# Folded wide cross attention in a two-layer decoder: scores issued three half tiles ahead in place of two

## The chip, the core and the metric

The kernel runs on one core of a Trainium2 chip. The metric is the device time of one execution, in microseconds. The engines are TensorE (PE, with PEld its weight loads), VectorE (DVE), ScalarE (ACT), GpSimd (POOL) and SyncE (SP, which issues the transfers). Each has its own instruction stream; they wait for one another by semaphores.

## What is computed

A decoder of two layers on x (4 batches of 512 tokens, 128 wide) with a context of 77 tokens per batch. Each layer is self attention, cross attention and a mixture of eight experts, and behind each an addition and a layer norm. The change lies in the cross attention of the second layer: 16 heads of 64 over the 77 context tokens.

```python
def _L1_xattn_ref(inputs_q, inputs_kv, Wq, bq, Wk, bk, Wv, bv, Wo, bo):
    q = jnp.einsum('bqm,mhd->bqhd', inputs_q, Wq) + bq
    k = jnp.einsum('bkm,mhd->bkhd', inputs_kv, Wk) + bk
    v = jnp.einsum('bkm,mhd->bkhd', inputs_kv, Wv) + bv
    q = q / jnp.sqrt(jnp.asarray(HD, q.dtype))
    attn = jax.nn.softmax(jnp.einsum('bqhd,bkhd->bhqk', q, k), axis=-1)
    out = jnp.einsum('bhqk,bkhd->bqhd', attn, v)
    return jnp.einsum('bqhd,hdm->bqm', out, Wo) + bo
...
x = _layernorm(x + _L1_xattn_ref(x, ctx_1024, ctx_1024, ...), axis=-1)
```

## The kernel before

`decoder` runs the stages one after another. Ahead of `flat_cross`, `wide_operands` has folded the projections: A holds for each batch and head Wq times the keys, CP the part that comes from the query bias (three bf16 parts), U the values times Wo. So scores are XT times A, and the output is the weights times U, with no projection of x in between.

`flat_cross` handles 16 tiles of 128 tokens (NT), each in two halves of eight heads (HH): 32 half tiles h, with tile t = h // 2 and batch t // 4. The program of each engine is written out without a loop on the chip, and its order is the order of the Python calls. For one half tile:

- PE `score(h)`: two groups of four heads, each a matmul of XT with A (L1876, f32, 308 columns) and one that adds CP (L1878), into the two banks of ps_s chosen by h % 2. Ahead of them it waits for `lessened` of h - 2, which read those banks.
- DVE `lessen(h)`: maximum of each head (L1961), then the subtraction from PSUM into PR[h % RING] (L1965). RING is 3, so it waits until PE has turned h - 3.
- ACT `exp(h)` (L1926), in place in PR.
- DVE `total(h)`: sum (L1972) and reciprocal (L1976).
- POOL `normalise(h)` (L1853): PR times the reciprocal, in place.
- PE `turn(h)`: five transposes of PR into the two banks of ps_t (L1886), after `normed` of h and `taken` of h - 1.
- ACT `take(h)` (L1932): ps_t into PT[h % 2].
- PE `weigh(h)`: PT times U into ps_v or ps_f by tile (L1896; the profile shows ten instructions for five matmuls).
- DVE `add(t)` (L1982): the output added to X, once per tile.

Once per batch the layer norm follows in the midst of the next batch: DVE `statistics` (L1986, L1989) in its iteration with h % 8 == 2, POOL `rstd` (L1847, L1849), DVE `apply` (L1995) in the iteration with h % 8 == 3, then PE `back` (L1904, four transposes of X into the first bank of ps_t, behind `s_n`) and ACT `columns` (L1939, from there to XT). Since `back` uses a bank of ps_t, the next turn waits for `s_xt`. The last batch's runs behind the loop.

What sets the order around the change is the order within each program: DVE's iteration h is lessen(h + 2), total(h + 1), the addition and the step of the layer norm; ACT's is take(h), exp(h + 2); POOL's is normalise(h), with rstd behind that of h % 8 == 3; PE's is in the lines below. SP issues one small load for this stage (L1830).

Of the kernel before, what the change touches and what calls it, by code (L numbers as in the profile page):

```python
# [14 lines left out]
QT = S // P  # L15
# [1767 lines left out]
def flat_cross(c, tag, A, CP, U, bo, pre=None):  # L1783
# [6 lines left out]
    HALVES = 2 * NT  # L1790
    HH = H // 2
    W = CHUNKS * P
    RING = 3
    norms = 1 if pre is None else 2
    with ExitStack() as own:
        ONES = c.sb(f"{tag}_ONES", [NPART, P], BF16, own)
        BO = c.sb(f"{tag}_BO", [P, P], F32, own)
        WB = c.sb(f"{tag}_WB", [P, 2], F32, own)
        PR = c.sb(f"{tag}_PR", [P, RING, W], F32, own)
        PT = c.sb(f"{tag}_PT", [P, 2, W], F32, own)  # L1800
# [14 lines left out]
        def heads(ap):  # L1815
            return ap.rearrange("p (h k) -> p h k", k=KC)
# [4 lines left out]
        def output(t):  # L1821
            return (c.ps_v, c.ps_f)[t % 2][:, (t // 2 % 4) * P:(t // 2 % 4 + 1) * P]
# [4 lines left out]
        with nc.Block() as block:  # L1827
            @block.sync
            def _(sp):
                sp.dma_start(BO[:, :], row(bo)).then_inc(s_w, 16)  # L1830
                if pre is not None:
                    sp.dma_start(WB[:, 0:1], col(pre[0])).then_inc(s_w, 16)
                    sp.dma_start(WB[:, 1:2], col(pre[1])).then_inc(s_w, 16)

            @block.gpsimd
            def _(pool):
# [14 lines left out]
                def normalise(h):  # L1851
                    pool.wait_ge(inverted, h + 1)
                    nc.gpsimd.tensor_tensor(  # L1853
                        heads(PR[:, h % RING, 0:HH * KC]), heads(PR[:, h % RING, 0:HH * KC]),
                        RDEN[:, h % 2, :].rearrange("p (h a) -> p h a", a=1).broadcast_to([P, HH, KC]),
# [10 lines left out]
            @block.tensor  # L1866
            def _(pe):
                def score(h):
                    t, half = h // 2, h % 2
                    b = t // QT  # L1870
                    if h >= 2:
                        pe.wait_ge(lessened, h - 1)
                    for q in range(2):
                        g = slice(half * HH + 4 * q, half * HH + 4 * q + 4)
                        dst = c.ps_s[:, 2 * (h % 2) + q, 0:4 * KC]
                        nc.tensor.matmul(dst, c.XT[:, t * P:(t + 1) * P], A[:, b, g, :].rearrange("p h k -> p (h k)"),  # L1876
                                         start=True, stop=False)
                        mm = nc.tensor.matmul(dst, ONES[:, :], CP[:, g, b, :], start=False, stop=True)  # L1878
                    mm.then_inc(scores, 1)

                def turn(h):
                    pe.wait_ge(normed, h + 1)
                    if h >= 1:
                        pe.wait_ge(taken, h)
                    for i in range(CHUNKS):
                        mm = nc.tensor.transpose(c.ps_t[:, i // 4, (i % 4) * P:(i % 4 + 1) * P],  # L1886
                                                 PR[:, h % RING, i * P:(i + 1) * P], c.ident[:, :])
                    mm.then_inc(turned, 1)

                def weigh(h):  # L1890
                    t, half = h // 2, h % 2
                    pe.wait_ge(taken, h + 1)
                    if half == 0 and t >= 2:
                        pe.wait_ge(summed_x, t - 1)
                    for i in range(CHUNKS):
                        mm = nc.tensor.matmul(output(t), PT[:, h % 2, i * P:(i + 1) * P], U[:, t // QT, half * CHUNKS + i, :],  # L1896
                                              start=(half == 0 and i == 0), stop=(half == 1 and i == CHUNKS - 1))
                    mm.then_inc(weighed, 1)

                def back(b):  # L1900
                    pe.wait_ge(s_n, QT * (b + 1))
                    for i in range(QT):
                        src = c.X[:, b * QT + i, :] if pre is None else R2[:, i, :]
                        mm = nc.tensor.transpose(c.ps_t[:, 0, i * P:(i + 1) * P], src, c.ident[:, :])  # L1904
                    mm.then_inc(s_back, 1)

                pe.wait_ge(s_ones, 1)
                pe.wait_ge(s_pad, 1)
                score(0)
                score(1)  # L1910
                for h in range(HALVES):
                    if h % (2 * QT) == 6 and h > 6:
                        pe.wait_ge(taken, h)
                        back(h // (2 * QT) - 1)
                        pe.wait_ge(s_xt, h // (2 * QT))
                    turn(h)
                    if h + 2 < HALVES:
                        score(h + 2)
                    weigh(h)
                back(B - 1)  # L1920

            @block.scalar
            def _(act):
                def exp(h):
                    act.wait_ge(lessened, h + 1)
                    nc.scalar.activation(PR[:, h % RING, 0:HH * KC], PR[:, h % RING, 0:HH * KC], ACT.Exp).then_inc(exped, 1)  # L1926

                def take(h):
                    act.wait_ge(turned, h + 1)
                    if h >= 2:  # L1930
                        act.wait_ge(weighed, h - 1)
                    nc.scalar.activation(PT[:, h % 2, :], c.ps_t[:, :, :].rearrange("p a n -> p (a n)")[:, 0:W],  # L1932
                                         ACT.Copy).then_inc(taken, 1)

                def columns(b):
                    act.wait_ge(s_back, b + 1)
                    dst, src = c.XT[:, b * S:(b + 1) * S], c.ps_t[:, 0, :]
                    if pre is None:
                        nc.scalar.activation(dst, src, ACT.Copy).then_inc(s_xt, 1)  # L1939
                    else:  # L1940
                        nc.scalar.activation(dst, src, ACT.Identity, bias=WB[:, 1:2], scale=WB[:, 0:1]).then_inc(s_xt, 1)

                act.wait_ge(s_w, n_w)
                exp(0)
                exp(1)
                for h in range(HALVES):
                    if h % (2 * QT) == 6 and h > 6:
                        columns(h // (2 * QT) - 1)
                    take(h)
                    if h + 2 < HALVES:  # L1950
                        exp(h + 2)
                columns(B - 1)

            @block.vector
            def _(dve):
                stat, done = Chain(s_stat), Chain(s_n)

                def lessen(h):
# [3 lines left out]
                    dve.wait_ge(maxed, h + 1)  # L1962
                    if h >= RING:
                        dve.wait_ge(turned, h - RING + 1)
                    nc.vector.tensor_tensor(  # L1965
# [332 lines left out]
def decoder(nc, a, out):  # L2298

    scratch = nc.dram_tensor("split_parts", (B, 2, P, NPART, S), BF16, kind="Internal").ap()  # L2300
    with ExitStack() as ctx:
# [29 lines left out]
        with ExitStack() as own:  # L2331
            A, CP, U = flat_operand_tiles(c, "e", own)
            wide_operands(c, "e", *(a[f"L1_xattn_{n}"] for n in ("Wq", "bq", "Wk", "bk", "Wv", "bv", "Wo")), A, CP, U)
            flat_cross(c, "e", A, CP, U, a["L1_xattn_bo"])
# [33 lines left out]
```

## Time and profile before

| | us |
|---|---|
| median of 3 runs | 2390.18 |
| lowest, highest | 2387.64, 2396.96 |
| the profiled execution: time | 2394.99 |
| its span | 2393.2 |
| busy in the span: PE, PEld | 1842.1, 1041.4 |
| DVE, ACT, POOL | 1385.4, 1035.7, 155.9 |

The mean granted clock of TensorE over the span is 0.866 of full. The folded cross attention runs from 1920 us (its first scores) to 2175 us in this span. Matmuls are pipelined and their ends are modelled: a busy PE isn't PE at its peak, and neighbouring groups can overlap by a little.

### The profile page before, as it was taken

How to read it: one execution, taken by the hardware profiler on the slowest of the kernel's cores; microseconds unless marked ns; L12 is line 12 of the kernel's file. 1: busy time of each engine (PE TensorE's matmuls, PEld its weight loads, DVE VectorE, ACT ScalarE, POOL GpSimd, SP SyncE). 2: the span in 40 equal slices, each digit the busy share in tenths (PEclk: the TensorE clock that was granted, in tenths of full speed). 3: DMA queues.
4: the chain of work that ended last, by engine and by line, in shares of the span. 5: the costliest groups of instructions: out<-in, count | busy, mean ns of one | idle time of the engine just before them, and what ended most of it. 6: DMA issues, size and time to landing. Idle time of an engine off the chain costs nothing. (4 is left out here: it accounts for less than half of the span.)

```text
span 2393.2 us, 33578 instructions
## 1 busy us (share of the span) xinstructions
PE 1842.1 (77%) x9665; PEld 1041.4 (44%) x9718; DVE 1385.4 (58%) x4754; ACT 1035.7 (43%) x1970; POOL 155.9 (7%) x281
## 2 busy tenths in 40 slices
PE   3277773873365867799949999999999677777997
PEld 2144442541022323577724444544444345455665
DVE  7398866656365754433358777777677433333445
ACT  3288861651054645334316556566556221111221
POOL 2000003001000000000020000000000021110000
PEclk7699995896588989899969999999999865766999
DMA  2543102402513110100010000000000100000000
GB/s 56 79 46 36 18 3 42 58 11 47 78 13 39 21 21 3 36 19 18 10 36 1 1 1 1 1 1 0 1 1 1 36 2 1 1 0 14 21 20 24
DMA packets 57636, 48.74 MB, mean 20 GB/s; under 512 B 12691, under 2 KB 53047, under 8 KB 57527
## 3 DMA queue, kind: packets, MB, share of 16 engines
q1 hardware_dynamic: 57527, 47.45, 12.5%
q8 instruction: 49, 0.80, 0.1%
q14 instruction: 60, 0.49, 0.1%
HBM read 38.30 MB, written 8.91 MB: 20 GB/s over the span
## 5 line engine op out<-in xcount | busy, mean ns | idle before, releaser
L1432 PE MATMUL ps_s<-d_KZ,d_Q 128*128 128x512 f32 x512 | 265.4, 601 | 16.1 <-issue 6.8
L1580 ACT ACTIVATE d_PR<-d_PR,d_NM 128x512 f32<-128x512 f32 x256 | 184.6, 721 | 189.8 <-DVE d_NM L1511 189.3
L557 DVE TENSOR_REDUCE c_NM<-ps_t 128x1 f32<-128x512 f32 x256 | 169.9, 688 | 99.2 <-PE ps_t L437 97.5
L1507 DVE CUSTOM_DVE_ANT_0 d_PR<-ps_s,d_BH 128x512 f32<-128x512 f32 x256 | 176.2, 688 | 61.6 <-PE ps_t L1440 44.7
L437 PE MATMUL ps_t<-KX,QX 96*128 (+1 forms) x256 | 107.6, 425 | 108.7 <-DVE c_IB L575 47.9
L1440 PEld LDWEIGHTS ps_t<-ident,d_PR 128*128 128x128 f32 x1024 | 121.4, 141 | 150.7 <-issue 132.5
L619 ACT ACTIVATE c_PT<-ps_s 128x1024 f32<-128x1024 f32 x128 | 130.4, 1024 | 128.6 <-PE ps_s L460 126.7
L2282 DVE SCALAR_TENSOR_TENSOR X<-ps_t,GATE,X 128x128 f32<-128x128 f32 x272 | 76.7, 344 | 184.2 <-PE ps_t L2207 184.2
L1587 ACT ACTIVATE d_PT<-ps_t 128x512 f32<-128x512 f32 x256 | 149.9, 586 | 50.7 <-PE ps_t L1440 49.0
L1440 PE MATMUL ps_t<-ident,d_PR 128*128 128x128 f32 x1024 | 156.4, 275 | 10.1 <-ACT d_PT L1587 8.1
L762 ACT ACTIVATE a_PR<-a_PR,a_NM 128x128 f32<-128x128 f32 (+3 forms) x256 | 129.8, 555 | 77.9 <-DVE a_NM L743 77.9
L672 PE MATMUL ps_t<-ident,a_PR 128*128 128x128 f32 x640 | 115.5, 290 | 50.4 <-ACT a_PT L686 38.0
L2244 ACT ACTIVATE f_HT<-ps_s,f_BE 128x512 f32<-128x512 f32 x128 | 87.8, 687 | 128.0 <-PE ps_s L2197 127.2
L2197 PE MATMUL ps_s<-XT,g_W 128*128 128x512 f32 x288 | 132.5, 603 | 2.4 <-DVE g_HT L2261 2.4
L1519 DVE TENSOR_SCALAR d_PR<-d_PR,d_RDEN 128x512 f32<-128x512 f32 x256 | 124.7, 487 | 9.0
L2207 PEld LDWEIGHTS ps_t<-f_W,f_HT 128*128 128x128 f32 x1024 | 119.2, 192 | 14.8 <-issue 14.6
L1452 PE MATMUL ps_v<-d_PT,d_VB 128*64 128x512 f32 x512 | 116.9, 598 | 5.6 <-ACT d_PT L1587 5.0
L2207 PE MATMUL ps_t<-f_W,f_HT 128*128 128x128 f32 x1024 | 119.3, 275 | 0.0
L2197 PE MATMUL ps_s<-XT,f_W 128*128 128x512 f32 x256 | 117.0, 601 | 0.0
L1961 DVE TENSOR_REDUCE e_M<-ps_s 128x8 f32<-128x616 f32 x32 | 25.6, 800 | 153.0 <-PE ps_s L1878 153.0
L672 PEld LDWEIGHTS ps_t<-ident,a_PR 128*128 128x128 f32 x640 | 70.3, 142 | 96.2 <-ACT a_PT L686 48.1
L437 PEld LDWEIGHTS ps_t<-KX,QX 96*128 (+1 forms) x256 | 25.0, 98 | 187.3 <-issue 105.9
(330 smaller groups left out, 3237.6 us busy)
## 6 DMA issues: line engine op xcount, KB each, us to landing
QX<-split_parts SPq DMA_DIRECT2D x108, 128.0 KB
KX<-split_parts SPq DMA_DIRECT2D x72, 128.0 KB
f_W<-in_L_ffn_w SPq DMA_DIRECT2D x16, 256.0 KB, 3.1
split_parts<-a_PARTS SPq DMA_DIRECT2D x8, 384.0 KB, 10.0
split_parts<-c_PARTS SPq DMA_DIRECT2D x8, 384.0 KB, 11.2
g_W<-in_L_ffn_w SPq DMA_DIRECT2D x24, 128.0 KB, 2.2
split_parts<-b_PARTS SPq DMA_DIRECT2D x4, 384.0 KB, 10.7
X<-in_x SPq DMA_DIRECT2D x4, 256.0 KB
```

The source lines that it names most:

```text
L437: nc.tensor.matmul(c.ps_t[:, i % 2, :], QX[0:SROWS, bass.ds(head, 1), qt * P:(qt + 1) * P], KX[0:SROWS, bass.ds(head, 1), :], start=True, ...
L557: nc.vector.tensor_reduce(NM[:, qt, j:j + 1], c.ps_t[:, i % 2, :], AX.X, ALU.max, negate=True).then_inc(maxed, 1)
L619: nc.scalar.activation(PT[:, half, j, :, :], c.ps_s[:, 2 * (j % 2):2 * (j % 2) + 2, :], ACT.Exp).then_inc(exped, 1)
L672: last = nc.tensor.transpose(c.ps_t[:, qt % 2, kt * P:(kt + 1) * P], PR[:, j % 2, qt, kt * P:(kt + 1) * P], c.ident[:, :])
L762: nc.scalar.activation(PR[:, j % 2, qt, 0:k], PR[:, j % 2, qt, 0:k], ACT.Exp, bias=NM[:, j % 2, qt:qt + 1]).then_inc(exped, 1)
L1432: nc.tensor.matmul(c.ps_s[:, qt % 2, :], Q[:, p % 2, qt * P:(qt + 1) * P], KZ[:, p % 2, i % 2, :], start=True, stop=True).then_inc(scores, 1)
L1440: mm = nc.tensor.transpose(c.ps_t[:, qt % 2, kt * P:(kt + 1) * P], PR[:, i % 2, qt, kt * P:(kt + 1) * P], c.ident[:, :])
L1507: nc.vector.tensor_tensor_reduce(out=PR[:, h % 2, qt, :], in0=c.ps_s[:, qt % 2, :], in1=BH[:, h, S - P - qt * P:2 * S - P - qt * P], scale ...
L1580: nc.scalar.activation(PR[:, h % 2, qt, :], PR[:, h % 2, qt, :], ACT.Exp, bias=NM[:, h % 2, qt:qt + 1], accum_out=DEN[:, h % 2, qt:qt + 1] ...
L1587: nc.scalar.activation(PT[:, i // 2 % 2, i % 2, :, qt * P:(qt + 1) * P], c.ps_t[:, qt % 2, :].rearrange("p (k q) -> p k q", q=P), ACT.Copy ...
L2197: nc.tensor.matmul(c.ps_s[:, ch, :], W[:, (ch % CH) * P:(ch % CH + 1) * P], c.XT[:, b * S:(b + 1) * S], start=True, stop=True).then_inc(s_ ...
L2207: mm = nc.tensor.matmul(c.ps_t[:, b % 2, q * P:(q + 1) * P], HT[:, b % 2, ch, q * P:(q + 1) * P], W2[i][:, ch, :], start=(ch == 0), stop=( ...
```

## The change

PE's program in `flat_cross` issues the scores three half tiles ahead of the turn. Three scores go ahead of the loop. In the loop score(h + 3) follows turn(h). `back` moves from the half tiles with h % 8 == 6 to those with h % 8 == 7; there score(h + 3) stands between `back` and the wait for `s_xt`, ahead of the turn. PE's wait for `taken` ahead of `back` goes. ACT's `columns` moves by one half tile too. The programs of DVE and POOL, the ring of three in PR and the banks stay.

```diff
+    LEAD = 3
...
+                def ahead(h):
+                    if h + LEAD < HALVES:
+                        score(h + LEAD)
...
-                score(0)
-                score(1)
+                for h in range(LEAD):
+                    score(h)
                 for h in range(HALVES):
-                    if h % (2 * QT) == 6 and h > 6:
-                        pe.wait_ge(taken, h)
+                    due = h % (2 * QT) == 7 and h > 7
+                    if due:
                         back(h // (2 * QT) - 1)
+                        ahead(h)
                         pe.wait_ge(s_xt, h // (2 * QT))
                     turn(h)
-                    if h + 2 < HALVES:
-                        score(h + 2)
+                    if not due:
+                        ahead(h)
                     weigh(h)
                 back(B - 1)
...
                 for h in range(HALVES):
-                    if h % (2 * QT) == 6 and h > 6:
+                    if h % (2 * QT) == 7 and h > 7:
                         columns(h // (2 * QT) - 1)
                     take(h)
```

## Rows read from the trace of the kernel before

**Rows 1.** The page's clock by 40 slices of the span, in tenths of full.

```profile
PEclk7699995896588989899969999999999865766999
```

**Rows 2.** Windows: length, busy us (instructions) per engine, PEclk, DMA share, GB/s.

```profile
120.00:320.00 200.00, 158.12 (x1184) 87.18 (x1202) 177.57 (x1015) 169.40 (x380) 10.53 (x52) 1.00 0.28 30
1280.00:1840.00 560.00, 533.32 (x2267) 267.33 (x2266) 403.23 (x1532) 334.56 (x769) 0.00 (x0) 1.00 0.00 1
1930.00:2153.00 223.00, 172.22 (x620) 111.38 (x620) 83.90 (x166) 42.41 (x60) 39.08 (x35) 0.64 0.00 0
2111.00:2151.00 40.00, 33.84 (x105) 21.53 (x104) 15.63 (x33) 7.01 (x10) 6.13 (x6) 0.50 0.00 1
```

**Rows 3.** Waits, 1930 to 2153 us: total us, times, longest.

```profile
DVE e_M L1961 <- PE ps_s L1878: 137.1, 29, 5.8
...
PE ps_t L1886 <- POOL e_PR L1853: 52.2, 28, 4.0
```

**Rows 4.** Timeline, half tile at 1.2 GHz: start, us, instruction [idle before <-releaser].

```profile
1938.08 1.33 PE L1886 MATMUL ps_t<-ident,e_PR 128*128 128x128 f32 x5 [1.52 <-POOL e_PR L1853]
...
1942.43 2.50 PE L1896 MATMUL ps_v<-e_U,e_PT 128*128 128x128 f32 x10
...
1946.46 1.33 PE L1886 MATMUL ps_t<-ident,e_PR 128*128 128x128 f32 x5 [1.53 <-POOL e_PR L1853]
```

**Rows 5.** Timeline, one half tile at 2.4 GHz.

```profile
2104.32 0.77 PE L1886 MATMUL ps_t<-ident,e_PR 128*128 128x128 f32 x5 [2.65 <-POOL e_PR L1853]
...
2105.12 0.70 ACT L1932 ACTIVATE e_PT<-ps_t 128x640 f32<-128x640 f32 x1 [2.34 <-PE ps_t L1886]
...
2106.72 1.38 PE L1896 MATMUL ps_f<-e_U,e_PT 128*128 128x128 f32 x10
2106.82 0.80 DVE L1961 TENSOR_REDUCE e_M<-ps_s 128x8 f32<-128x616 f32 x1 [3.70 <-PE ps_s L1878]
2107.66 0.80 DVE L1965 TENSOR_TENSOR e_PR<-ps_s,e_M 128x616 f32<-128x616 f32 x1
...
2109.19 0.20 DVE L1976 RECIPROCAL e_RDEN<-e_DEN 128x8 f32<-128x8 f32 x1
2109.47 1.22 POOL L1853 TENSOR_TENSOR e_PR<-e_PR,e_RDEN 128x616 f32<-128x616 f32 x1 [5.21 <-DVE e_RDEN L1976]
...
2110.75 0.47 PE L1886 MATMUL ps_t<-ident,e_PR 128*128 128x128 f32 x1 [2.65 <-POOL e_PR L1853]
```

**Rows 6.** Timeline: turn(0), turn(29) and weigh(31), the last.

```profile
1929.71 1.33 PE L1886 MATMUL ps_t<-ident,e_PR 128*128 128x128 f32 x5 [3.96 <-POOL e_PR L1853]
...
2152.63 0.77 PE L1886 MATMUL ps_t<-ident,e_PR 128*128 128x128 f32 x5 [1.69 <-POOL e_PR L1853]
...
2166.30 2.50 PE L1896 MATMUL ps_f<-e_U,e_PT 128*128 128x128 f32 x10 [0.79 <-ACT e_PT L1932]
```

**Rows 7.** Timeline: DVE beside POOL (first three) and alone (the last).

```profile
1922.74 4.93 POOL L1842 TENSOR_TENSOR X<-X,e_BO 128x512 f32<-128x512 f32 x4 [2.59 <-DMA e_BO<-in_L_xattn_bo]
1923.24 0.80 DVE L1965 TENSOR_TENSOR e_PR<-ps_s,e_M 128x616 f32<-128x616 f32 x1
...
2142.82 1.98 DVE L1995 TENSOR_SCALAR X<-X,e_MV,e_RS 128x128 f32<-128x128 f32 x4
...
2171.92 1.11 DVE L1995 TENSOR_SCALAR X<-X,e_MV,e_RS 128x128 f32<-128x128 f32 x4 [1.48 <-POOL e_RS L1849]
```

**Rows 8.** Timeline: back's transposes, the addition to X, the statistics.

```profile
2096.09 0.60 PE L1904 MATMUL ps_t<-ident,X 128*128 128x128 f32 x4
...
2102.89 0.24 DVE L1982 TENSOR_TENSOR X<-X,ps_v 128x128 f32<-128x128 f32 x1
...
2155.78 2.50 PE L1896 MATMUL ps_v<-e_U,e_PT 128*128 128x128 f32 x10
2158.07 1.06 PE L1904 MATMUL ps_t<-ident,X 128*128 128x128 f32 x4
...
2169.16 0.87 DVE L1986 BATCH_NORM_STATS2 e_ST<-X 128x6 f32<-128x128 f32 x4
```

## The prediction, made before the changed kernel was run

> **What bounds the kernel now.** I read first the clock line of the slices [rows 1]: before and after the last fifth of the span the granted TensorE clock is at or near full, in the slices of the folded cross attention it is six tenths or so. The windows say what belongs to that [rows 2]: over 1930 to 2153 us TensorE is busy 172.22 of 223 us and every other engine much less (DVE 83.90, ACT 42.41, POOL 39.08), at a mean clock of 0.64. No engine is full, so a chain of waits sets the pace. The waits name it [rows 3]: DVE's maximum waits for PE's scores, 137.1 us in 29 waits, and PE's turn waits for POOL's normalise, 52.2 us in 28.
>
> One half tile at 2.4 GHz shows the chain in order [rows 5]. turn(h) starts at 2104.32, the scores of h+2 follow it, DVE's reduce of them starts at 2106.82, its subtraction, the sum of the *previous* half tile and the reciprocal end at 2109.39, POOL normalises from 2109.47 for 1.22 us, and turn(h+1) starts at 2110.75: 6.43 us. The link is DVE's program order: total(h+1) stands behind lessen(h+2), and lessen(h+2) needs score(h+2), which PE issues only behind turn(h). So the whole chain is walked once for every half tile, and PE waits 2.65 us of 6.43. At 1.2 GHz the same chain takes 8.38 us, of which PE waits 1.53 [rows 4]: PE's part of it is longer, the rest the same. From turn(0) at 1929.71 to turn(29) at 2152.63 it is 222.92 us, 7.69 us for each of 29 half tiles [rows 6], between the two.
>
> **The issue three ahead.** score(h+3) is now issued behind turn(h), so score(h+2) is already there when DVE comes to lessen(h+2). Is its bank free? score(h+3) waits for lessen(h+1), which stands ahead of total(h) on DVE, and turn(h) had to wait for the normalise behind total(h): always fulfilled, and the weigh and turn behind it on PE are not held. Is the ring free? lessen(h+2) writes the slot of h-1 and waits for turn(h-1), which PE issued before score(h+2). So the chain turn(h), score(h+3), lessen(h+3), total(h+2), normalise(h+2), turn(h+2) is as long as before, 6.43 us at 2.4 GHz and 8.38 at 1.2, but spans two half tiles: 3.2 and 4.2 us for each. That is no longer the bound.
>
> **What is late next.** PE itself. At 2.4 GHz it works 6.43 - 2.65 = 3.78 us per half tile [rows 5]; groups overlap a little when they follow without a gap: at 1.2 GHz a weigh of 2.50 us is followed after 2.29 by the next transposes, 0.21 less [rows 8], and I take half of that at 2.4. So 3.68 us at 2.4, and 8.38 - 1.53 - 0.21 = 6.64 at 1.2 [rows 4]. DVE needs from the reduce to the reciprocal's end 2.57 us, half an addition to X of 0.24, and an eighth of statistics (0.87, and the aggregates behind them taken as 0.4) and apply (1.98), 0.41: 3.1 us [rows 5, 7, 8]. It stays under PE, in the mean. Once per batch, though, statistics and apply come in successive half tiles; DVE has about 1 us spare per half tile and the chain another 2 x 3.68 - 6.43 = 0.9 per two, so 1.3 and then 1.98 us cost perhaps 0.2 at a time; 0.5 in all. ACT has 0.70 for the take and about as much for the exponential, POOL 1.22.
>
> **The clock.** This is the largest term, and not in the diff. In this trace TensorE runs at 1.00 wherever it works with small gaps: 1280 to 1840 with 533.32 us busy of 560, and even 120 to 320 with only 158.12 of 200 [rows 2]. In the changed stage the clock falls behind waits of 1.5 to 2.65 us that come back every half tile; these waits go. I take 2.4 GHz for it, except for three half tiles at the start: the clock had fallen before 1929.71 and the stage starts at 1.2 [rows 4, 6]. The unknown is how soon it rises, bounded from both sides by rows: from the first half tile, or not at all (below).
> The Trainium skill says the same in "TensorE: Matmul & The Clock Gate", section "HAM oscillation — how this bites in real kernels": pauses between groups of matmuls send the clock back down again and again. By that rule alone the whole stage would be at 2.4 GHz, some 2271 us; the trace agrees with it in the direction only, as in one stretch of 40 us PE was busy 33.84 us and stayed at 1.2 [rows 2].
>
> **Start.** score(2) goes before the loop, waits for lessen(0) and runs while PE had been idle 3.96 us before turn(0) [rows 6]. turn(0) waits for POOL, so it stays at 1929.71: nothing gained, nothing lost.
>
> **Back, moved from the seventh to the eighth half tile of a batch.** Its transposes took 0.60 us at 2.4 GHz [rows 8]; before they lay in PE's wait, now PE has no wait to cover them. ACT's copy to XT lies beside score(h+3), which is placed between for that. But then turn(7) and weigh(7) stand next to each other with no scores between, and the take is exposed: it starts 0.80 us behind the turn's start and lasts 0.70 [rows 5], so some 0.9 us of wait. 1.45 us each, three times: 4.4 us. The wait for `taken` that is removed was fulfilled anyway: weigh(h-1) waits for it. On ACT the columns copy moves with it and holds one take. No DMA is moved, and SP's queue has nothing in this stage but its first load.
>
> **Sum, on the profiled execution.** From turn(0): 3 x 6.64 = 19.9; 26 x 3.68 = 95.7; the last three half tiles have no scores and each takes turn, take, weigh: 0.80 + 0.70 + 0.05 + 1.38 - 0.1 = 2.83 (at 1.2 before, 4.35), so 8.5; back 4.4; DVE 0.5. Together 129.0, so the last weigh ends at 2058.7 in place of 2166.30 + 2.50 = 2168.8 [rows 6]: 110.1 less, and 0.5 in the last transposes at 2.4. That is 110.6. The profiled execution had a span of 2393.2 and a time of 2394.99, 4.8 above the median: 2284.4 on its scale, **2279.6 from the median of 2390.18**, and I say 2280.
>
> **Rivals.**
> 1. The dense stream doesn't raise the clock. For it: at 1.2 GHz PE was busy 6.85 of 8.38 us and stayed there from 2111 to 2151 us [rows 2, 4], and one half tile of the new stream has the same work. Wholly at 1.2: 29 x 6.64 + 3 x 4.4 + 3 x 2 = 212, ending at 2141.6, 27 less: 2363. Half of it at 1.2 (11.5 half tiles more, 2.96 each): 34 more than forecast, 2314. Against it: the rows of 120 to 320.
> 2. DVE against GpSimd. Before, the normalise ran while DVE had nothing to do; now it lies beside DVE's work. The apply beside a normalise took 1.98 us for four, without one 1.11 [rows 7]. If DVE lost the whole 1.22 us in each half tile, it would need 4.3 us and be the bound: 26 x 0.64 = 17 more, 2296. Against it: the subtraction beside POOL's addition took 0.80 [rows 7], as it does alone [rows 5].
> The Trainium skill has this rule in "SBUF — State Buffer", section "Who interferes with whom": GpSimd and VectorE share a pair of ports, which VectorE takes with two inputs from SBUF or in a two-port mode. The subtraction and the reductions read their large input from PSUM or have one input; the apply is the case that it covers, and the trace agrees (1.98 against 1.11).
> 3. Slower: the same lock, hit by every one of DVE's four instructions. Each would wait a whole normalise, 4 x 1.22 = 4.9, so 8.0 us per half tile; 29 x (8.0 - 7.69) = 9 more: 2399, and up to some 2470 if the additions and the layer's instructions lost as much. It decides from 4.6 us of blocking per half tile. Only one normalise per half tile exists and the rows show no such thing.
> 4. The change doesn't do what it says: the bank's or the ring's wait ties the chain to one half tile again. Then 7.69 stays: about 2390. The order above speaks against it.
>
> **How the numbers follow.** Forecast (2266 to 2290) 0.65; clock in part at 1.2 (2290 to 2330) 0.14; wholly at 1.2, 2363: 0.07; DVE the bound, about 2296: 0.09; no effect 0.03; slower 0.02. The low end is the forecast with no half tile at 1.2 (3 x 2.96 = 9 less) and the spread of the three runs (2.5 below their median): 2268, rounded down to 2266; the high end takes in DVE as the bound and half the stage at 1.2: 2316. Within 0.5% of 2390 is about what a measurement of this kernel can't tell from no change. Faster by more: 0.95; within: 0.03; slower: 0.02.
>
> **What would show it.** Right: turn to turn at 3.7 us, PE's wait for POOL's normalise nearly gone, DVE's maximum not waiting for L1878 but starting at once, clock over 0.9 from 1940 on, three pauses of about 1 us in the half tiles with back. Wrong: PE without waits but matmuls of L1896 at 2.50 us per ten (rival 1); DVE reduces or subtractions well over 0.80 us (rivals 2, 3); turn to turn still 6.4 or 8.4 us (rival 4). The prediction fails most if the clock isn't given: it carries 83 of the 110 us.

## The result and the profile after

The changed kernel takes 2274.64 us (median of 4 runs, 2269.94 to 2278.58), the one before beside it 2393.18 (2387.64 to 2396.96): ratio 0.9506, 95% interval 0.9474 to 0.9537. It is faster by 118.5 us between the medians. The profiled execution took 2271.61 us with a span of 2269.9, 123.4 less than the profiled one of before.

The page's clock of the changed kernel, by 40 slices; the folded cross attention begins in the 34th:

```profile
PEclk7599996696659889889996999999999987998999
```

The windows answer to [rows 2]: the loop from turn(0) to turn(29), and a piece of it without a back (length, busy us of PE, PEld, DVE, ACT, POOL, PEclk, DMA share, GB/s).

```profile
1926.00:2037.00 111.00, 109.09 (x617) 74.28 (x617) 83.61 (x168) 39.49 (x60) 38.77 (x36) 0.96 0.00 1
1941.00:1973.00 32.00, 32.00 (x191) 21.89 (x190) 24.91 (x52) 11.78 (x18) 12.20 (x11) 1.00 0.00 1
```

PE is busy in 109 of 111 us, where it was in 172 of 223, and the mean clock is 0.96 in place of 0.64. DVE's busy time is what it was, 83.6 us, in half the time.

The waits answer to [rows 3] (total, times, longest). First DVE's from 1930 to 2046 us, then all waits of PE in the same stretch:

```profile
DVE e_M L1967 <- PE ps_s L1879: 24.4, 20, 3.1
```

```profile
PE ps_f L1897 <- ACT e_PT L1938: 3.2, 4, 0.8
PE ps_v L1897 <- ACT e_PT L1938: 0.8, 1, 0.8
PE ps_t L1887 <- ACT XT L1945: 0.7, 1, 0.7
```

PE's wait for the normalise, 52.2 us in 28 before, is not in this list any more. What is left is the exposed take, five times 0.8 us (three at a back, two in the last half tiles without scores), and one wait for XT. One half tile in the timeline answers to [rows 5]:

```profile
1944.39 0.71 PE L1887 MATMUL ps_t<-ident,e_PR 128*128 128x128 f32 x5
...
1945.64 0.20 DVE L1982 RECIPROCAL e_RDEN<-e_DEN 128x8 f32<-128x8 f32 x1
...
1945.93 1.22 POOL L1854 TENSOR_TENSOR e_PR<-e_PR,e_RDEN 128x616 f32<-128x616 f32 x1 [2.35 <-DVE e_RDEN L1982]
...
1946.73 1.38 PE L1897 MATMUL ps_v<-e_U,e_PT 128*128 128x128 f32 x10
1946.84 0.80 DVE L1967 TENSOR_REDUCE e_M<-ps_s 128x8 f32<-128x616 f32 x1 [0.84 <-PE ps_s L1879]
1947.67 0.80 DVE L1971 TENSOR_TENSOR e_PR<-ps_s,e_M 128x616 f32<-128x616 f32 x1
...
1947.95 0.71 PE L1887 MATMUL ps_t<-ident,e_PR 128*128 128x128 f32 x5
```

Turn to turn (from the start of one turn to the start of the next) is 1947.95 - 1944.39 = 3.56 us. The normalise of the next half tile ends at 1947.15 and the turn starts at 1947.95, with no idle time noted: PE has come to its own bound, with 0.8 us to spare in the chain. DVE's maximum still waits, here 0.84 us and 24.4 in all in place of 137.1, but for scores that are three ahead, and PE issues those without a pause.

### The profile page after: what moved, and what is told of

Same layout as the page of the kernel before. It is cut to its first block and busy times, and to the rows that moved or that the text cites. A ratio compares the mean times of both kernels' runs of the same rounds, so it can differ in the third digit from the quotient of the medians.

```text
span 2269.9 us, 33575 instructions
## 1 busy us (share of the span) xinstructions
PE 1775.7 (78%) x9665; PEld 1000.7 (44%) x9718; DVE 1384.8 (61%) x4754; ACT 1032.5 (45%) x1970; POOL 155.7 (7%) x281
## 5 line engine op out<-in xcount | busy, mean ns | idle before, releaser
L2213 PEld LDWEIGHTS ps_t<-f_W,f_HT 128*128 128x128 f32 x1024 | 119.2, 192 | 14.8 <-issue 14.6
L2248 ACT ACTIVATE g_GT<-ps_s 128x512 f32<-128x512 f32 x72 | 43.0, 597 | 141.9 <-PE ps_s L2203 141.8
```

Of the source, the lines that this page charges most:

```text
L2213: mm = nc.tensor.matmul(c.ps_t[:, b % 2, q * P:(q + 1) * P], HT[:, b % 2, ch, q * P:(q + 1) * P], W2[i][:, ch, :], start=(ch == 0), stop=( ...
```

## The experiments

Each was run beside the kernel before, on one chip per group; ratios are to that. Turn to turn is read off the timeline of the profiled execution.

**One: the lead of two again, all else of the change kept.**

```diff
-    LEAD = 3
+    LEAD = 2
```

> The changed kernel with a lead of two again: only the placement of back in the eighth half tile is new. If the gain is the third half tile of lead, turn to turn goes back to 6.43 us at 2.4 GHz and 8.38 at 1.2, PE waits for the normalise in each half tile, and the time is 2388 to 2400, as before. If the placement of back or the dropped wait had a part in it, it lies below 2380.

2383.7 us, ratio 0.9993 (0.9958 to 1.0029). Most half tiles take 6.4 to 8.4 us again, and from turn(0) to turn(29) it is 209.7 us at a mean clock of 0.72. That this is 13 us less than the 222.92 of the kernel before, at 0.64, is no gain: the profiled execution of the kernel before took 2394.99 us, on the longer side of its 13 executions in this group (2371.2 to 2406.31), and the ratio has 1 in its interval. So the clock of this chain is not one number; it differs from one execution to the next. So the moved back and the dropped wait carry nothing that can be seen, and within this change the whole gain hangs on the lead. The median is below the range that I gave, but so is that of the kernel before beside it (2383.16).

**Two: the lead of three, back where it was.**

```diff
-                    due = h % (2 * QT) == 7 and h > 7
-                    if due:
+                    if h % (2 * QT) == 6 and h > 6:
                         back(h // (2 * QT) - 1)
-                        ahead(h)
                         pe.wait_ge(s_xt, h // (2 * QT))
                     turn(h)
-                    if not due:
-                        ahead(h)
+                    ahead(h)
                     weigh(h)
```

(and `columns` on ACT likewise.)

> The changed kernel with back in the seventh half tile, where it was before, and the turn, the scores and the weigh behind it in the usual order. The lead stays three. If the move of back carries nothing, the time is that of the changed kernel, 2270 to 2279; by the trace each back should cost PE 0.5 us of transposes and some 0.7 us of wait for the copy to XT (as the third one did, 0.69), in place of 1.45 us in all: 0 to 1 us less over the stage. The rival, that back has to stand in the eighth half tile for the lead to work, gives waits of PE of over 2 us at each back and at least 5 us more.

2270.72 us, ratio 0.9498 (0.9436 to 0.9561): as fast as the changed kernel. PE around the first back:

```profile
1977.39 1.38 PE L1897 MATMUL ps_v<-e_U,e_PT 128*128 128x128 f32 x10
1978.61 0.60 PE L1909 MATMUL ps_t<-ident,X 128*128 128x128 f32 x4
1979.89 0.33 PE L1887 MATMUL ps_t<-ident,e_PR 128*128 128x128 f32 x1 [0.69 <-ACT XT L1942]
```

From back's start to the turn it is 1.28 us, near the 0.5 and 0.7 that were expected; in the changed kernel the same thing costs 1.45. The move was not needed for the lead and costs slightly more than leaving back in place, too little to be seen in the time.

**Three: the kernel before, lead two, with the sum first on DVE.**

```diff
                 for h in range(HALVES):
-                    if h + 2 < HALVES:
-                        lessen(h + 2)
                     if h + 1 < HALVES:
                         total(h + 1)
+                    if h + 2 < HALVES:
+                        lessen(h + 2)
```

> The kernel before, lead two, with one edit on DVE: the sum of h+1 stands ahead of the maximum and subtraction of h+2. If DVE's order was the link that made the chain span one half tile only, this alone nearly does it: the chain is turn, scores (2.50 us), maximum and subtraction (1.63), exponential (0.8), sum and reciprocal (1.0), normalise (1.3), 7.3 us for two half tiles, 3.65 each, about PE's own 3.56. So 2272 to 2290. The rival, that only scores issued earlier can do it, expects about 2390.

2278.29 us, ratio 0.9528 (0.9464 to 0.9591). Turn to turn is 3.62 and 3.68 us by turns, 4.5 to 5.4 where the layer norm's steps and back come in. Four rows in place of the chain, at one half tile:

```profile
1944.73 0.80 DVE L1961 TENSOR_REDUCE e_M<-ps_s 128x8 f32<-128x616 f32 x1 [1.12 <-PE ps_s L1878]
...
1946.39 0.72 ACT L1926 ACTIVATE e_PR<-e_PR 128x616 f32<-128x616 f32 x1 [2.67 <-DVE e_PR L1965]
...
1947.14 0.79 DVE L1972 TENSOR_REDUCE e_DEN<-e_PR 128x8 f32<-128x616 f32 x1 [0.78 <-ACT e_PR L1926]
...
1948.25 1.22 POOL L1853 TENSOR_TENSOR e_PR<-e_PR,e_RDEN 128x616 f32<-128x616 f32 x1 [3.35 <-DVE e_RDEN L1976]
```

One and the same half tile goes through maximum, exponential, sum and normalise, and the chain spans two turns. This is the strongest evidence for the reading of the kernel before: what bound it was neither the lead of two by itself nor a short ring, both of which stayed here, but that on DVE a sum that was ready stood behind a maximum that wasn't. Two remedies exist, an earlier score or a later maximum, and each gives nearly all of the gain alone.

**Four: the kernel before, with useless work in part of PE's waits.**

```diff
+                def fill(h):
+                    for i in range(4):
+                        nc.tensor.matmul(c.ps_t[:, 1, P:2 * P], PT[:, h % 2, i * P:(i + 1) * P], U[:, h // (2 * QT), i, :],
+                                         start=True, stop=True)
...
                     weigh(h)
+                    fill(h)
```

> The kernel before with four more matmuls of the weigh's kind behind each weigh, into a part of PSUM that nobody reads: work without use, in PE's wait. The chain is not shortened. At 1.2 GHz they take 2.0 us, 0.5 more than the wait of 1.5; at 2.4 GHz 1.1 of 2.65. If the clock falls because of the waits, the filled stage runs at 2.4 GHz nearly throughout and turn to turn is 6.43 us in place of 7.69: 29 x 1.26 = 36 us less, about 2355, though PE has more to do. If the clock doesn't follow from PE's waits, the stage stays at about 0.64 and the time is 2390 to 2400.

2358.01 us, ratio 0.987 (0.9805 to 0.9936): a kernel with more work on its busiest engine, faster by 1.3%. The window from turn(0) to turn(29):

```profile
1922.00:2115.00 193.00, 150.36 (x853) 108.25 (x853) 83.85 (x166) 42.38 (x60) 39.02 (x35) 0.92 0.00 1
```

And PE's rows at one half tile, with the filling (L1902) and what is left of the wait behind it:

```profile
1952.29 1.38 PE L1896 MATMUL ps_v<-e_U,e_PT 128*128 128x128 f32 x10
1953.51 1.06 PE L1902 MATMUL ps_t<-e_U,e_PT 128*128 128x128 f32 x8
1956.32 0.77 PE L1886 MATMUL ps_t<-ident,e_PR 128*128 128x128 f32 x5 [1.75 <-POOL e_PR L1853]
```

The clock is 0.92 in place of 0.64 (0.72 in the profiled execution of one, which has the same chain), most half tiles take 6.42 or 6.43 us, and the 29 of them 192.7 in place of 222.9: 30 us less, of 36 expected, as a few half tiles still ran at 1.2 GHz. Against one's 209.7 it is 17 less, and the medians differ by 25. PE still waits 1.75 us in most half tiles, in place of 2.65 at the same clock [rows 5]. So filling a third of PE's wait brings most of the clock back, with the chain untouched. Whether the shorter wait or the added work does it, this run can't tell; eight adds waits and no work for PE.

**Five: back's transposes between the scores and the weigh of the seventh half tile**, lead three.

```diff
-                    due = h % (2 * QT) == 7 and h > 7
-                    if due:
-                        back(h // (2 * QT) - 1)
-                        ahead(h)
+                    if h % (2 * QT) == 7 and h > 7:
                         pe.wait_ge(s_xt, h // (2 * QT))
                     turn(h)
-                    if not due:
-                        ahead(h)
+                    ahead(h)
+                    if h % (2 * QT) == 6 and h > 6:
+                        pe.wait_ge(taken, h + 1)
+                        back(h // (2 * QT) - 1)
                     weigh(h)
```

(the wait for `s_xt` stays ahead of the next turn; back at the head of the eighth half tile goes.)

> Lead three, with back's transposes between the scores and the weigh of the seventh half tile: the take of that half tile is long done, and ACT's copy to XT (0.60 us and 0.1 of semaphores) lies beside weigh (1.25 us at 2.4 GHz). Each back then costs PE its 0.5 us of transposes alone, in place of 1.45 (changed kernel) or 1.3 (back in the seventh half tile, ahead of the turn). So the two half tiles around it take 7.6 us together, and the stage is 3 x 0.9 = 2.7 us shorter than in the changed kernel: 2267 to 2276, not told from it by time alone. The rival, that ACT's copy is still waited for, gives over 1 us each.

2269.0 us, ratio 0.9502 (0.9442 to 0.9563). In the profiled execution the turn behind a back comes 3.96 us after the one before, 0.40 over the usual 3.56; no wait for XT is left. So back costs 0.4 in place of 1.45 us, as expected within 0.1; the time alone doesn't tell it from the changed kernel.

```profile
1995.31 0.66 PE L1909 MATMUL ps_t<-ident,X 128*128 128x128 f32 x4
...
1995.80 1.28 PE L1897 MATMUL ps_f<-e_U,e_PT 128*128 128x128 f32 x10
1996.00 0.60 ACT L1944 ACTIVATE XT<-ps_t 128x512 f32<-128x512 f32 x1 [0.98 <-PE ps_t L1909]
...
1996.92 0.71 PE L1887 MATMUL ps_t<-ident,e_PR 128*128 128x128 f32 x5
```

**Six: the changed kernel with DVE's maximum taken three times.**

```diff
+                    for i in range(2):
+                        nc.vector.reduce_max(m, score_banks(h), AX.X).then_inc(maxed, 1)
+                        dve.wait_ge(maxed, 3 * h + i + 1)
                     nc.vector.reduce_max(m, score_banks(h), AX.X).then_inc(maxed, 1)
-                    dve.wait_ge(maxed, h + 1)
+                    dve.wait_ge(maxed, 3 * h + 3)
```

> The changed kernel with DVE's maximum taken three times into the same place: two times 0.83 us more in each half tile, work without use. DVE needs 3.1 + 1.7 = 4.8 us per half tile and becomes the bound in place of PE (3.56). Turn to turn 4.7 to 4.9, PE waits some 1.2 us each time: 29 x 1.25 = 36 us more than the changed kernel, about 2310. If waits of that size already bring the clock down, PE's part of the half tile is up to 6.64 us and the time goes to 2320 to 2360.

2299.82 us, ratio 0.9637 (0.9575 to 0.97), some 10 us under the 2310 that I expected. From turn(0) to turn(29) it took 133.5 us, 4.60 for each, 22 more than the changed kernel where 36 were expected. DVE is the bound:

```profile
1929.00:2063.00 134.00, 114.89 (x619) 75.43 (x620) 127.48 (x225) 42.04 (x60) 39.10 (x36) 0.96 0.00 1
```

127.48 / 29 = 4.40 us of DVE per half tile. My 3.1 us for the changed kernel was too much, its trace has 83.61 / 29 = 2.88: I had spread the layer norm's steps over eight half tiles, where three batches' steps fall into 29, and had counted the short gaps between DVE's instructions as work; that accounts for most of the 0.2. The usual half tile, 4.10 and 4.30 us, shows it without the layer norm. The clock stays at 0.96, with waits of PE of 0.32 and 0.53 us in a usual half tile and up to 2.3 where the layer norm's steps come in.

**Seven: five, and the sum first on DVE.** The edit of five, and

```diff
-                    if h + 2 < HALVES:
-                        lessen(h + 2)
                     if h + 1 < HALVES:
                         total(h + 1)
+                    if h + 2 < HALVES:
+                        lessen(h + 2)
```

> The same as with back's transposes under the weigh, and on DVE the sum of h+1 ahead of the maximum of h+2 as well. If PE is the bound at 3.56 us, shortening the chain again brings only what the layer norm's steps cost (0.36 us per batch): 1 us less, the same time, 2266 to 2275. The rival, that the chain still holds part of each half tile, expects turn to turn under 3.5 us and 5 us or more less.

2264.38 us, ratio 0.9476 (0.9415 to 0.9537), the lowest median of all; it is 1.6 us below the range that I gave and 4.6 below five, whose executions overlap with it. Turn to turn stays 3.56 us, now in the half tiles behind the layer norm's steps too (3.87 and 3.61 in five), and never less as long as there are scores to issue. That speaks against the rival: behind the start the chain has no part in the time any more.

**Eight: the maximum five times.** The edit is that of six, with four maxima more in place of two:

```diff
+                    for i in range(4):
+                        nc.vector.reduce_max(m, score_banks(h), AX.X).then_inc(maxed, 1)
+                        dve.wait_ge(maxed, 5 * h + i + 1)
                     nc.vector.reduce_max(m, score_banks(h), AX.X).then_inc(maxed, 1)
-                    dve.wait_ge(maxed, h + 1)
+                    dve.wait_ge(maxed, 5 * h + 5)
```

> The changed kernel with DVE's maximum taken five times: four times 0.83 us more. With three, turn to turn was 4.10 and 4.30 us in turn (DVE the bound) and the clock stayed at 0.96 with waits of PE of some 0.6 us. Here DVE needs 5.9 us, so PE at 2.4 GHz waits 2.3 us in each half tile, as in the kernel before (1.6 to 2.65). If waits of that size bring the clock down, it is well below 0.96 here in spite of the lead of three, PE at 1.2 GHz (6.64 us) becomes the bound by turns, and turn to turn lies between 5.9 and 6.7: 2345 to 2375. If the clock follows from something else that the lead brought, it stays over 0.9, turn to turn 5.8 to 6.0 and with the layer norm's steps 6.2 in the mean: 2340 to 2350.

2352.04 us, ratio 0.987 (0.9842 to 0.9898).

```profile
1931.00:2111.00 180.00, 137.96 (x620) 89.65 (x621) 173.88 (x283) 42.37 (x60) 39.30 (x36) 0.82 0.00 1
```

```profile
PE ps_t L1887 <- POOL e_PR L1854: 43.8, 24, 3.6
```

From turn(0) to turn(29) 179.4 us, 6.19 each. PE has the same work as in the changed kernel and longer waits, and the clock is down from 0.96 to 0.82 with the scores three ahead, so it isn't the lead that keeps it up but what the lead does to PE's waits. The second row is PE's wait for the normalise: 1.8 us in the mean, up to 3.6. The lower clock costs little time here, since DVE (5.8 to 6.0 us in a usual half tile) sets the pace either way.

**Nine: seven with the lead of two.**

```diff
-    LEAD = 3
+    LEAD = 2
```

> The fastest version so far (2264 us; lead three, back's transposes under the weigh, sum first on DVE) with the lead at two again. The chain of 7.3 us for two half tiles is then as long as PE's work, 3.65 against 3.56 us each: 29 x 0.09 = 3 us more in the half tiles, and once per batch the layer norm's steps on DVE come into the chain (4.47 to 4.6 and 5.4 us where it was tried without the move of back), some 3 x 1.5 us more: 2268 to 2278. The rival, that the lead does nothing once DVE's order is mended, expects no difference, with turn to turn at 3.56.

2275.27 us, ratio 0.9555 (0.9525 to 0.9586), 11 more than seven, whose runs were of another group (the two intervals overlap). Turn to turn 3.62 and 3.68, and 4.48 and 5.42 at the layer norm's steps; from turn(0) to turn(29) 114.6 us against 108.4. With DVE's order mended the lead is worth 6 us in this stage.

## Why the prediction was right

2280 us was forecast, in a range of 2266 to 2316; 2274.64 was measured. By its steps:

- **The chain and its link.** Right. Its place on DVE is shown by three: with the sum first the lead of two runs at 3.65 us, the value worked out from the rows.
- **The reading of the clock line.** Too generous: outside this stage the slices 2, 7, 10, 11 and 21 of [rows 1] show five or six tenths, so "at or near full" doesn't hold for all of them. Nothing in the sum rests on it; the two windows at 1.00 [rows 2] are as stated.
- **What is late next: PE.** Right. PE's half tile is 3.56 us, not 3.68: I had taken 0.1 us of overlap between groups, and the trace has 0.16 behind the weigh (1.38 long, the turn 1.22 behind its start) and 0.06 more in the transposes (0.71 for 0.77). That is 26 x 0.12 = 3.1 us.
- **The clock.** Right, and the largest term. Only two half tiles were slow at the start, 6.64 and 4.56 us, then 3.57: 14.8 for the first three in place of 19.9, 5.1 us less. Four shows that filling part of PE's waits with other work raises the clock with the chain as it was, eight that longer waits lower it under a lead of three too. The Trainium skill's rule ("TensorE: Matmul & The Clock Gate", "HAM oscillation — how this bites in real kernels"), that pauses between groups of matmuls bring the clock down, agrees with both in the direction: 0.92 with the pauses filled in part, 0.82 with them put back. The page's example is of pauses for DMA; here they were waits for another engine.
- **Start.** Right but for 0.3 us. From the stage's first transfer to turn(0) it took 10.14 us, 9.86 before; score(2) fills the wait and PE waits 0.57 us in place of 3.96.
- **Back.** 1.45 us each was forecast. From the back at 1983.92 to the second turn behind it at 1988.93 it is 5.01 us, 3.56 + 1.45. The third back, in the last half tile, has no scores left to put under the copy and waits 0.69 us for XT; its take is exposed with or without it, and the last three half tiles took 9.72 us with it, 9.95 forecast.
- **The layer norm's steps on DVE.** 0.2 us at a time were forecast and 0.36 came: the turns behind the apply are at 3.86 and 3.62 us, twice (the third time 3.87, and then a half tile without scores). There the chain still shows: the normalise from 1975.47 on ends at 1976.69 and the turn starts at 1976.74, where 1.22 us behind the weigh's start, as in the usual half tile, would be 1976.44. Small in either case, and gone in seven.

```profile
1975.22 1.38 PE L1897 MATMUL ps_v<-e_U,e_PT 128*128 128x128 f32 x10
...
1975.47 1.22 POOL L1854 TENSOR_TENSOR e_PR<-e_PR,e_RDEN 128x616 f32<-128x616 f32 x1 [3.15 <-DVE e_RDEN L1982]
...
1976.74 0.77 PE L1887 MATMUL ps_t<-ident,e_PR 128*128 128x128 f32 x5
```

- **The tail.** 0.5 us less was forecast; it didn't come. PE waits 4.3 us for the last layer norm; the weigh ahead of that wait took 1.38 us, as at 2.4 GHz, the transposes behind it 1.11 us, as at 1.2, so the clock fell in between.
- **DVE against GpSimd.** The rival didn't happen. The subtraction and the reductions kept their 0.80 and 0.78 us beside the normalise; only the apply did not:

```profile
1970.94 1.97 DVE L2001 TENSOR_SCALAR X<-X,e_MV,e_RS 128x128 f32<-128x128 f32 x4
1971.10 1.22 POOL L1854 TENSOR_TENSOR e_PR<-e_PR,e_RDEN 128x616 f32<-128x616 f32 x1 [1.10 <-DVE e_RDEN L1982]
```

  1.97 us, and 1.98 in [rows 7]; POOL kept its 1.22.
- **The other rivals.** The bank's and the ring's waits tied nothing: no wait of PE for `lessened` shows, and turn to turn is 3.56.
- **The signs.** One was wrong: DVE's maximum was to start at once, and it waits for the scores, 24.4 us in 20 waits. Since PE is the bound, whoever needs its scores waits for them; in six, where DVE is the bound, it waited 2.4 us in all. The others came as named.

The sum closes. From turn(0) to the end of the last weigh it was 239.1 us and is 2047.07 - 1926.06 = 121.0, 118.1 less where 110.1 were forecast; the 8 us are the 3.1 and the 5.1 above, and small ones against each other. The rest of the 123.4 us between the two profiled executions lies in code that the change doesn't touch, 3.9 us in the stages ahead and 1.6 behind, less the 0.3 that the start took longer. The start of this stage lay anywhere from 1912.7 to 1928.5 us in the profiled executions here, with the same code ahead of it. The forecast of the time was only 5 us off for a reason that is luck: 110.6 us of gain were forecast and the medians differ by 118.5, 8 more, but the forecast set out from a median of 2390.18, and beside the change the kernel before measured 2393.18, 3 more.

How the gain divides between chain and clock can't be said as a sum, since each needs the other. With most of the clock back and the chain as it was, the loop is 30 us shorter between the profiled executions and the time 25 between the medians (four). With the chain mended and the clock at 1.2 GHz throughout it would be 27 us shorter by the working of the prediction; no run held the clock down, so that is only argued. Both together give 118.

## What to carry to other kernels

When an engine waits in each step of a pipeline that looks deep enough, write down each engine's program order around the wait: an instruction that is ready may stand behind one that is not, and then two stages of the pipeline are tied into one. Issuing the producer earlier and moving the ready instruction forward cure the same fault, and here neither needed another buffer. A regular wait of PE of the size seen here can cost twice, by itself and by the clock that falls behind it (waits of 0.3 to 0.5 us did not have that second cost), so a change that removes the waits is worth more than their length, and its price is best worked out at 2.4 GHz with one or two slow steps at the start.

## What the runs showed of the hardware that was not expected

Work without use made a kernel faster. 128 more matmuls of 128 columns in PE's waits, 32 x 1.06 = 34 us of PE's time at 2.4 GHz, took 25 us off the median, since they raised the granted clock of the stage from 0.64 or 0.72 (the kernel before and one) to 0.92. It took little: waits of 1.75 us in most half tiles were still there. With 0.32 to 0.53 us in the usual half tile (six) the clock was 0.96, with 1.8 in the mean and up to 3.6 (eight) 0.82, with 1.5 to 2.65 (the kernel before) 0.64. The length of the waits alone does not order these four, and what does was not found.
